# A two-layer block on one core: the low half of the second FFN product in seven half-width products, and x1 added to the output by DMA

## The reference, cut to what matters

```python
uv = layernorm(x) @ in_proj_w + in_proj_b;  u, v = uv[..., :D], uv[..., D:]
y = scan(a * h + b * conv3(silu(v)))             # along the rows, per column
h = (u * silu(y)) @ out_proj_w + out_proj_b + layernorm(x)
x = x + layernorm(layernorm(h) * ln_w + ln_b)    # this x is called x1 below
f = gelu(layernorm(x) @ ternary(W1).T + b1) @ ternary(W2).T + b2
x = x + layernorm(f)
```

## Time and profile before

| what | value |
|---|---|
| median of 3 runs | 1427.58 us (1425.25 to 1428.63) |
| the profiled execution | 1427.88 us, of which its span 1425.9 us |
| PE busy | 1403.4 us (98%) |
| DVE busy | 1119.8 us (79%) |
| ACT busy | 911.8 us (64%) |
| POOL busy | 414.2 us (29%) |
| granted TensorE clock | full in all 40 slices |

### The profile page before, as it was taken

One profiled execution on the slowest core, in us unless ns is written; L12 is line 12 of the kernel. 1 busy time (PEld: TensorE's weight loads), 2 busy tenths in 40 slices (PEclk: granted clock), 3 DMA queues, 4 the chain that ended last, 5 costly groups with the idle time before them and its releaser, 6 DMA issues.

```text
span 1425.9 us, 23101 instructions
## 1 busy us (share of the span) xinstructions
PE 1403.4 (98%) x8426; PEld 825.4 (58%) x8426; DVE 1119.8 (79%) x1889; ACT 911.8 (64%) x1504; POOL 414.2 (29%) x522
## 2 busy tenths in 40 slices
PE   6999999999999999999999999999999999999998
PEld 4444556656566564666646566565665646655664
DVE  8999987878779686786868778687786867998744
ACT  7998675657666565675656757476665756753553
POOL 5234241322413232142421413224132321422211
PEclk9999999999999999999999999999999999999999
DMA  8703320311311122111311203113121221001200
GB/s 248 257 27 85 65 78 17 86 30 31 89 30 60 31 53 67 31 60 31 89 31 31 74 17 89 31 30 89 23 67 30 53 67 31 31 1 30 60 30 30
DMA packets 156001, 82.26 MB, mean 58 GB/s; under 512 B 132720, under 2 KB 132720, under 8 KB 155760
## 3 DMA queue, kind: packets, MB, share of 16 engines
q1 hardware_dynamic: 155888, 80.79, 22.4%
HBM read 31.49 MB, written 16.78 MB: 34 GB/s over the span
## 4 chain that ended last, share of the span: by engine, by line
PE 86%; DVE 4%; issue 2%; DMA 0%; ACT 0%; POOL 0%; POOLq 0%; DVEq 0%; ACTq 0%
PE f1b L573 14%; PE f1b L574 14%; PE f2b L597 14%; PE f2b L599 14%; PE misc L538 6%; PE misc L536 6%; PE misc L537 6%; PE misc L550 3%; PE misc L552 3%; PE misc L551 3%; PE f2b L622 1%; PE f2b L621 1%; DVE w L1234 0%; DVE g_lo L949 0%; DMA xs<-x_dram 0%
## 5 line engine op out<-in xcount | busy, mean ns | idle before, releaser
L573 PE MATMUL f1b<-x3T,w 128*128 128x256 f16 x1792 | 397.5, 273 | 0.0
L574 PE MATMUL f1b<-x3T,w 128*128 128x256 f16 x1792 | 397.5, 273 | 0.0
L597 PE MATMUL f2b<-w,ring 128*128 128x512 fp8e5 x960 | 363.9, 379 | 0.8 <-DVE ring L847 0.8
L599 PE MATMUL f2b<-w,ring 128*128 128x512 fp8e5 x960 | 363.8, 379 | 0.0
L1652 ACT ACTIVATE ring<-f1b,par 128x256 f32<-128x256 f32 x480 | 201.2, 471 | 227.0 <-PE f1b L574 226.7
L2088 POOL TENSOR_SCALAR ve<-mv 128x4 f32<-128x4 f32 (+2 forms) x89 | 35.2, 395 | 729.8 <-DVE mv L839 729.7
L847 DVE SCALAR_TENSOR_TENSOR ring<-ring,f_sc 128x512 f16<-128x512 f32 x256 | 200.4, 796 | 30.1 <-ACT ring L1666 30.0
L574 PEld LDWEIGHTS f1b<-x3T,w 128*128 128x128 fp8e5 x1792 | 175.4, 98 | 32.6
L573 PEld LDWEIGHTS f1b<-x3T,w 128*128 128x128 fp8e5 x1792 | 175.3, 98 | 32.5
L1666 ACT ACTIVATE ring<-ring,f_sc 128x512 f16<-128x512 f32 x256 | 182.0, 718 | 0.0
L536 PE MATMUL misc<-x1T,win_hi 128*128 128x512 f16 x456 | 172.8, 379 | 0.0
(11 more groups left out here) (233 smaller groups left out, 2143.4 us busy)
## 6 DMA issues: line engine op xcount, KB each, us to landing
out_dram<-hb SPq DMA_DIRECT2D x64, 256.0 KB, 2.0
xs<-x_dram SPq DMA_DIRECT2D x14, 1024.0 KB, 6.0
ring<-w1t_dram SPq DMA_DIRECT2D x3, 1024.0 KB, 13.5
stage<-w2t_dram SPq DMA_DIRECT2D x3, 1024.0 KB, 8.2
x1T<-tp SPq DMA_TRANSPOSE x68, 3.1
xs<-x_dram SPq DMA_DIRECT2D x4, 256.0 KB, 3.6
stage<-w_in_dram SPq DMA_DIRECT2D x4, 256.0 KB, 5.0
xs<-x_dram SPq DMA_DIRECT2D x2, 512.0 KB, 6.6
```

The lines of the kernel that those rows point to most:

```text
L573: pe.matmul(o_, w, src[:, k, h * TH:(h + 1) * TH], start=k == 0, stop=False)
L574: mm = pe.matmul(o_, w, src[:, KC + k, h * TH:(h + 1) * TH], start=False, stop=k == KC - 1)
L597: pe.matmul(f2b[q][:, :], h_hi[:, i % H_SLOTS, qs], w2[:, chunk, :], start=chunk == 0, stop=False)
L599: mm = pe.matmul(f2b[q][:, :], h_lo[:, i % H_SLOTS, qs], w2[:, chunk, :], start=False, stop=chunk == FC - 1)
```

## The change

Three things change, two of them for tiles 2 to 13 alone.

First, the lo half of f2. A unit's lo product is a 2 x 2 by 2 x 2 block product: two blocks of 128 rows by two hidden chunks, times two chunks by two halves of 256 output columns. Before, it is 8 block products, run as 4 matmuls of 512 columns. After, it is Winograd's form with 7 products, run as 7 matmuls of 256 columns. It needs four sums and differences of the h_lo blocks (`presums`, on VectorE, for two units together, each of its 4 operations 128 x 256 in f16), four combinations of w2 blocks (`combine`, 8 operations once, in step 3), and a longer way out of PSUM (`drain`: 7 operations for each half of a tile in place of 2 `f_add`). The seven products of a half use all four banks, so the next half waits until `drain` has emptied them. The h = 0 half is therefore drained among the `h_add`s of its own step, and f2(8) moves from before the output projection to behind f1(12).

Second, x1 is stored to the output by SP (`store_x1`, behind the transposes of x3), and `finish` becomes a DMA issued by GpSimd that adds the normed FFN result to it in memory.

Third, tap 0 of the convolution moves on VectorE from the start of a step to the end of the step before (`AT_TAP0_NEXT`), and its wait for the right edge moves to tap 2.

```diff
+AT_TAP0_NEXT = (17.41, 17.42, 17.43, 17.44)
+AT_PRESUM, AT_PRESUM_LAST = .005, .01
+AT_COMBINED = (7.65, 7.66, 11.65, 11.66, 14.65, 17.5, 17.51, 17.52)
...
+    def seven(t):
+        return 1 < t < NT - 2
...
                 if t >= X_SLOTS:
-                    sp.wait_ge(fin_ok, NB * (t - X_SLOTS + 1))
+                    sp.wait_ge(n3_ok, NB * (t - X_SLOTS + 1))
+                    for j in range(NB):
+                        sp.wait_ge(x1_st[j], 16 * (t - X_SLOTS + 1))
...
+                sp.dma_start(out_d[t, j], xs[:, t % X_SLOTS, j, :]).then_inc(x1_st[j], 16)
...
+            def f2_seven(t, j):
+                i, (h, chunks) = FC * t + j, unit(j)
+                p, r = chunks[0], i % H_SLOTS
+                if p == 0:
+                    pe.wait_ge(f_ok, NB * t + 2 * h)
...
+                pe.wait_ge(hh_ok, i + 1)
+                for q in range(2):
+                    for n, chunk in enumerate(chunks):
+                        pe.matmul(f2b[q][:, :], h_hi[:, r, n * TH + q * P:n * TH + (q + 1) * P], w2[:, chunk, :],
+                                  start=p == 0 and n == 0, stop=False, skip_group_check=True)
+                pe.wait_ge(sums_ok, 4 * rank(i) + 4)
...
+                product(f2b[2], left, a11, w2[:, p, left], p == 0)
+                product(f2b[0], left, a12, w2[:, p + PAIRS, left])
+                product(f2b[3], right, s1, t1, p == 0)
+                product(f2b[2], right, s2, t2)
+                product(f2b[3], left, s3, t3)
+                product(f2b[0], right, s4, w2[:, p + PAIRS, right])
+                product(f2b[1], left, a22, t4).then_inc(f2_mm, 1)
...
+                mid = min(half(s), PAIRS) if seven(fa or 0) else half(s)
...
-                        if j >= half(s) + LAG:
+                        if j >= mid + LAG:
                             f2(fa, j - LAG)
...
+            def presums(t, j, last):
...
+                if last:
+                    ve_.wait_ge(sums_ok, k + 3)
+                    ve_.tensor_tensor(s4, a12, s2, ALU.subtract).then_inc(sums_ok, 1)
+                    return
+                ve_.wait_ge(hl_ok, i + 2)
+                ve_.wait_ge(f2_mm, i - 2)
+                ve_.tensor_tensor(s3, a11, a21, ALU.subtract).then_inc(sums_ok, 1)
+                ve_.tensor_tensor(s1, a21, a22, ALU.add).then_inc(sums_ok, 1)
+                ve_.wait_ge(sums_ok, k + 1)
+                ve_.tensor_tensor(s2, a22, s3, ALU.subtract).then_inc(sums_ok, 1)
...
+                return [first, second, third, fourth, fifth, lambda: block_(0), lambda: block_(1)]
...
                     for j in range(NB):
                         h_add(c, j)
+                        for part in parts[2 * j:2 * j + 2]:
+                            part()
...
             def finish(e, j):
                 pool.wait_ge(fn_ok, NB * e + j + 1)
-                pool.tensor_tensor(hb[:, j, :], hb[:, j, :], xs[:, e % X_SLOTS, j, :], ALU.add).then_inc(fin_ok, 1)
+                pool.wait_ge(x1_st[j], 16 * (e + 1))
+                pool.dma_start(out_d[e, j], fo(e, j), accum_op=ALU.add).then_inc(out_st[j], 16)
```

More of the change, by code:

```diff
@@ L472, in _ @@
             transpose("t3", 1, 3)
+            store_x1(0)
             for s in range(3, NT + 2):
                 _, c, n, e = tiles(s)
-                if e is not None:
-                    for j in range(NB):
-                        store(e, j)
-                    if e + X_SLOTS < NT:
-                        load_x(e + X_SLOTS)
+                if e is not None and e + X_SLOTS < NT:
+                    load_x(e + X_SLOTS)
+                if s == 3:
+                    store_x1(1)
                 if n is not None:
@@ L483, in _ @@
                     transposes("t3", c)
+                if c is not None and c < NT - 1:
+                    store_x1(c)
             for j in range(NB):
-                store(NT - 1, j)
+                store_last(j)
             for j in range(NB):
-                sp.wait_ge(out_st[j], 16 * NT)
+                sp.wait_ge(x1_st[j], 16 * (NT - 1))
+                sp.wait_ge(out_st[j], 16 * (NT - 1))
+                sp.wait_ge(last_st[j], 16)
         @block.tensor
@@ L780, in _ @@
                             f2(fa, j - lag)
-                left = [lambda j=j: f2(fa, j) for j in range(half(s) - LAG, half(s))] if fa is not None and s < NT else []
+                mid = min(half(s), PAIRS) if seven(fa or 0) else half(s)
+                left = [lambda j=j: f2(fa, j) for j in range(half(s) - LAG, mid)] if fa is not None and s < NT else []
                 if c is not None and s < NT:
@@ new lines, in lows, with drain, part, first @@
+            def lows(t, js, at):
+                items = [(at[j], lambda j=j: lo(t, j)) for j in js]
+                if seven(t):
+                    pairs = [j for j in js if j % 2 == 1]
+                    items += [(at[j] + AT_PRESUM, lambda j=j: presums(t, j - 1, False)) for j in pairs]
+                    items += [(at[j] + AT_PRESUM_LAST, lambda j=j: presums(t, j - 1, True)) for j in pairs]
+                return items
+            def drain(t, h):
+                dst, k = fo_pair(t, h), 5 * (2 * (t - 2) + h)
+                quarter = dst.rearrange("p j (n c) -> p (j n) c", c=TH)
+                left, right = slice(0, TH), slice(TH, 2 * TH)
+                def part(src, cols, out_, in1):
+                    ve_.scalar_tensor_tensor(out=out_, in0=src[:, cols], scalar=f_inv[:, 0:1], in1=in1,
+                                             op0=ALU.mult, op1=ALU.add).then_inc(part_ok, 1)
+                def first():
+                    ve_.wait_ge(f2_mm, half_done(t, h))
+                    ve_.wait_ge(step_ok, 1)
+                    for j in range(2 * h, 2 * h + 2):
+                        if h == 1:
+                            ve_.wait_ge(x3_lo, NB * (t + 1) + j + 1)
+                        elif seven(t - 1):
+                            ve_.wait_ge(out_st[j], 16 * t)
+                    part(f2b[2], left, quarter[:, 0, :], b2_row[:, 0:TH])
+                def second():
+                    part(f2b[3], right, quarter[:, 3, :], b2_step[:, :])
+                def third():
+                    ve_.wait_ge(part_ok, k + 1)
+                    part(f2b[2], right, quarter[:, 1, :], quarter[:, 0, :])
+                def fourth():
+                    ve_.wait_ge(part_ok, k + 3)
+                    part(f2b[3], left, quarter[:, 2, :], quarter[:, 1, :])
+                def fifth():
+                    ve_.wait_ge(part_ok, k + 4)
+                    ve_.tensor_tensor(dst[:, :, right], quarter[:, 1:3, :],
+                                      quarter[:, 3:4, :].to_broadcast([P, 2, TH]), ALU.add).then_inc(part_ok, 1)
+                def block_(q):
+                    ve_.wait_ge(part_ok, k + 5)
+                    ve_.scalar_tensor_tensor(out=dst[:, q, :], in0=f2b[q][:, :], scalar=f_inv[:, 0:1], in1=dst[:, q, :],
+                                             op0=ALU.mult, op1=ALU.add).then_inc(f_ok, 1)
+                return [first, second, third, fourth, fifth, lambda: block_(0), lambda: block_(1)]
@@ L898, in taps @@
                     ve_.wait_ge(tap0, i + 1)
+                    if c > 0 and b == 0:
+                        ve_.wait_ge(right_ok, c + 1)
                     if c == 0 and b < KC - 1:
@@ L1559, in _ @@
                     at_lo = AT_LO_PAIR if s == NT else AT_LO
-                    items += [(at_lo[j] if j < len(at_lo) else 1.2 + j, lambda j=j: lo(fa, j))
-                              for j in range(half(s))]
+                    items += lows(fa, range(half(s)), [at_lo[j] if j < len(at_lo) else 1.2 + j for j in range(FC)])
                 run(items)
@@ L1588, in _ @@
                 if c is not None:
+                    parts = drain(fa, 0) if seven(fa) else []
                     for j in range(NB):
                         h_add(c, j)
+                        for part in parts[2 * j:2 * j + 2]:
+                            part()
                         if s == NT - 1:
```

104 lines of the change are left out of this document (82 added, 22 removed).

## The result

The changed kernel takes 1497.36 us, the median of 4 runs (1494.88 to 1501.60), against 1426.41 for the kernel before (1425.05 to 1428.63): a ratio of 1.0499, 95% interval 1.0469 to 1.0529. It is slower. The profiled execution is 1498.6 us with a span of 1496.8; before it was 1427.88 with 1425.9. The 70.9 us between the spans are what has to be explained.

What follows compares the result with a forecast made beforehand. TensorE's queue of matmuls was taken to bound the kernel, any wait in it showing in full. 1427.9 + 32 (ten steps) + 6.6 (step 4) + 11 (step of tiles 13 and 14) = 1477.5, given as 1477 us; range 1441 to 1505.

Steps and rivals of the forecast that it cites:

- The sign: Slower, chance 0.86; carried by f2(4), which waits 2.4 to 2.5 us for lo(5)'s sums, held by d_conv(3).
- The other waits: TensorE in a steady step: o(2) 1.3 us, f2(8) 0.7, f2(10) 0.2, f2(0) 0.1, next f1(0) none.
- The saving: TensorE's lo half of f2: seven shorter matmuls save 0.10 us a unit, 1.6 a step, 19 over 12 tiles.
- Rival (d): Lo products: 256 columns with f16 stationary operand start over 0.123 us apart, saving nothing; +19, 1497 us; chance 0.04.
- VectorE's prices: VectorE operations: presum 0.29 us, 128x256 out of PSUM 0.45, combination 1.2; VectorE's sum 76.7 us a step.
- The odd steps: Step 4: f2(0) waits 3.4 us more, +6.6; step of tiles 13 and 14: VectorE has nothing spare, +11.
- The start: The stretch at the kernel's start, for which the prediction booked nothing.
- The step that failed: Steady step: 4.8 us of waits against 1.6 saved, a step of 89.9, +3.2; ten steps +32.
- (a): The forecast itself: TensorE waits at f2(4), o(2) and f2(8), 1461 to 1505 us; chance 0.67.
- (b): Only f2(4) waits in full; o(2) and later waits are absorbed, about 1441 us; chance 0.12.
- (c): Faster: VectorE reaches lo(5) before 711.8, so f2(4)'s wait goes; 1424.5 or 1409 us; chance 0.11.
- the 4 us given back: VectorE, 701 to 709 us: without GpSimd's four additions 4.0 us come back, but do not help f2(4).

Runs made afterwards that it cites:

- experiment 3: Changed kernel with lo(5) and the presums of units 4 and 5 put ahead of scans 2 and 3 on VectorE; 1453.98 us, ratio 1.0200.
- experiment 9: Changed kernel, seven products for tiles 3 to 12 only, lo(5) and h_add(0) earlier, late f2 delayed, low parts in VectorE's idle time; 1412.43 us, ratio 0.9908.
- experiment 1: Kernel before with f2(4) of tiles 2 to 13 also waiting for lo(5), nothing else changed; 1457.83 us, ratio 1.0226.
- experiment 10: Kernel before with f2(4) of tiles 2 to 13 waiting for y of the last column block, a shorter wait; 1446.57 us, ratio 1.0146.
- Experiment 8: Changed kernel with GpSimd's addition and SP's store put back in place of the adding DMA and x1's store; 1503.72 us, ratio 1.0545.
- experiment 11: Kernel before with f2(4) waiting for lo(5) and f2(2) waiting for tap 2 of the last column block; 1491.12 us, ratio 1.0452.
- experiment 12: Kernel before with f2(4) waiting for lo(5) and six more 512-column matmuls of u in each of 12 steps; 1486.51 us, ratio 1.0434.

## Why the prediction was right and where it was not

**The sign, and what carries it.** Right. f2(4) waits for VectorE's last presum 12 times. f1(0) at 717.32 puts scan 3's end of waiting at 738.75, 21.4 later (21.1 predicted), held by d_conv(3) as argued; lo(5) starts 23.9 later (23.7), the sums are there at 25.7 (25.5). The wait shown is 2.31 (2.4 to 2.5), and 2.52 as experiment 3 takes it out.

**The other waits.** o(2) 1.16 (1.3), f2(8) 0.41 (0.7), f2(10) 0.17 (0.2), f2(0) none (0.1), f1(0) none. Together 4.05 shown. By the steps of experiment 9 and of after at full clock it is 90.06 - 85.07 = 4.99 in the queue (4.8 predicted): experiments 1 and 10 show that a wait costs 0.16 more than its row says, 4 x 0.16 = 0.64, and 0.3 stay unplaced. The 0.16 is in how the row counts: idle time begins at the modelled end of the matmul before, 0.38 behind its start, where in a stream the next starts 0.215 behind it. The step at full clock is 90.06 (89.9).

**The saving.** 1.58 a step (1.6). Rival (d), whose 1497 is the measured time, is out: the seven products start 0.11 apart, and experiment 9 collects the whole saving.

**VectorE's prices.** A presum is 284 to 292 ns (0.29, the middle of two ends far apart), an f32 part of the drain out of PSUM at 128x256 474 to 479 (0.45), a combination 1.21 (1.2). For the presum the estimate from the Trainium skill (VectorE: DVE Perf Modes, section Mode 2×_1P), 0.28, came out as well. VectorE is busy 75.76 of a step of 91.72 (76.7 predicted):

```profile
717.32:809.04 91.72, 87.61 (x578) 56.51 (x576) 75.76 (x155) 54.94 (x92) 20.21 (x30) 0.98 0.27 58
```

With GpSimd's additions gone a lo is 738 ns in place of 796, though GpSimd's queue now makes descriptors for the adding DMAs. In the trace of after the 18 lo that run beside the issue of such a DMA take 730 ns on average and the other 238 739. That is the half of the Trainium skill's rule (SBUF — State Buffer, section Who interferes with whom) that no row before could show, and it holds here. Experiment 8 shows the other half on the presums themselves, by form, where GpSimd adds again; three of the four presums go to 401 to 406, one stays at 292:

```profile
L964 DVE TENSOR_TENSOR stage<-ring 128x256 f16<-128x256 f16 x96 | 39.0, 406 | 0.0
```

**The odd steps.** Step 4 was +8.0 at full clock (6.6): its f2(0) waits 4.86, where 3.4 were said. The step of tiles 13 and 14 and all behind it comes to +10.3 at full clock (11). The start is 1.6 us shorter, booked at nothing; the wait of 2.24 us for an h_add at 125.55 is not there, but by experiments 1, 10, 11 and 12 that is how one execution differs from another.

**The step that failed.** "Together 2.5 + 1.3 + 0.7 + 0.2 + 0.1 = 4.8 of waits against 1.6 saved: a step of 89.9, +3.2." The waits in that sum are right to 0.3 each; the sum takes a wait to cost its own length. It costs 1.67 us more each time TensorE's clock is lowered behind it. Twelve times in the profiled execution that is 20 us, what is missing between 1477 and 1497. The trace of before could not give the price, with its clock at 1.00 up to TensorE's last matmul. Its longest wait past 165 us was 0.8 us. It does hold one of 2.24 us, at 125.55, ahead of the stretch that I looked at, and the clock stayed full behind it; experiment 3 shows that the same wait can go the other way. One harmless case was no ground to put twelve at nothing: that was a term to bound, and it was left out. That the range held the time is luck, since its upper end was made for a slower presum.

**Rivals.** (a) happened in its waits; that the time lies near its upper end has another reason, the clock. (b) did not: o(2) and f2(8) waited. (c) did not: VectorE waits 2.09 us before scan 3, with the 4 us given back in hand. Experiment 3 shows what (c) would have needed, lo(5) ahead of the scans, and even then the other waits leave it 2% slower.
